# Last stage of a fused token mixer, retention and attention kernel: probabilities turned on VectorE in 32 by 32 blocks, value products in sixteen 32 by 32 tiles

## The reference

```python
x = layernorm(h)
gating = softmax(x @ W_gate.T)                       # 16 gates per token
idx, top1 = argmax(gating), max(gating)
q, k, v = split(x @ W_qkv.T, 3)
k_shared = k of head idx                             # (batch, 192, 32)
v_shared = top1 * (v of head idx)                    # (batch, 192, 32)
att = einsum('bhqd,bkd->bhqk', q, k_shared) / sqrt(32)
att = softmax(where(key <= query, att, -inf))
y = einsum('bhqk,bkd->bhqd', att, v_shared)
h = h + y.transpose(0, 2, 1, 3).reshape(batch, 192, 512)
```

## Time and profile before

| | |
|---|---|
| median of three runs | 1273.48 us |
| profiled execution, its own time | 1273.32 us |
| its span, first to last instruction | 1271.5 us |
| mean granted TensorE clock | 0.988 |
| busy share of the span: matmuls, weight loads, VectorE, ScalarE, GpSimd | 93, 77, 61, 44, 41% |
| one middle pair of the last stage, scores to scores | 52.3 us |

### The profile page before, as it was taken

One profiled execution on the slowest core, in us unless ns is written; L12 is line 12 of the kernel. 1 busy time (PEld: TensorE's weight loads), 2 busy tenths in 40 slices (PEclk: granted clock), 3 DMA queues, 4 the chain that ended last, 5 costly groups with the idle time before them and its releaser, 6 DMA issues. The chain is left out here.

```text
span 1271.5 us, 21324 instructions
## 1 busy us (share of the span) xinstructions
PE 1187.6 (93%) x7408; PEld 976.5 (77%) x7408; DVE 770.4 (61%) x1483; ACT 564.8 (44%) x1777; POOL 517.7 (41%) x714
## 2 busy tenths in 40 slices
PE   1689999999999999789999999998999999999997
PEld 1577788787887888678788887787887888888875
DVE  7897867678676742265555555634555655656544
ACT  6334333444424422253333333314556565565656
POOL 3576766747758651243233333302223212132131
PEclk9988999999999999989999999999999999999998
DMA  6022223222222222995667654133625527256061
GB/s 270 26 91 91 99 100 116 92 91 100 109 108 91 108 100 91 300 289 165 187 208 220 186 166 133 59 75 67 133 53 117 121 47 166 60 109 141 7 137 35
DMA packets 63354, 154.69 MB, mean 122 GB/s; under 512 B 9616, under 2 KB 26128, under 8 KB 61712
## 3 DMA queue, kind: packets, MB, share of 16 engines
q1 hardware_dynamic: 63248, 153.33, 41.3%
HBM read 67.19 MB, written 56.62 MB: 97 GB/s over the span
## 5 line engine op out<-in xcount | busy, mean ns | idle before, releaser
L1815 ACT ACTIVATE probs<-psum,row_max 128x128 f32<-128x128 f32 (+1 forms) x384 | 143.2, 389 | 41.5 <-DVE row_max L1984 29.2
L1119 ACT ACTIVATE square_scratch<-psum 128x128 f32<-128x128 f32 x192 | 51.0, 278 | 145.8 <-PE psum L1355 145.8
L1984 DVE TENSOR_REDUCE row_max<-psum 128x2 f32<-128x384 f32 (+1 forms) x128 | 79.1, 618 | 59.3 <-PE psum L2220 35.7
L2114 POOL TENSOR_TENSOR h_rows<-h_rows,y_normed 128x512 f32<-128x512 f32 x24 | 30.8, 1283 | 203.8 <-DVE y_normed L2000 203.8
L2091 POOL TENSOR_TENSOR picked_rows<-picked_rows 128x768 f32<-128x768 f32 (+1 forms) x64 | 61.4, 960 | 98.6 <-DVE picked_rows L1966 94.8
L753 POOL TENSOR_TENSOR stage<-stage 128x512 f32<-128x512 f32 x48 | 81.1, 1709 | 37.5 <-DVE stage L629 37.5
L1295 POOL TENSOR_TENSOR rr<-ss,consts_r 128x3 f32<-128x3 f32 x64 | 14.8, 231 | 188.6 <-ACT square_scratch L1119 184.0
L1991 DVE COPY raw_f<-psum 128x512 f32<-128x512 f32 x64 | 44.3, 692 | 70.2 <-PE psum L2233 70.2
L1815 ACT ACTIVATION_READ_ACCUMULATOR probs<-psum,row_max 128x1 f32 x384 | 80.9, 211 | 0.0
L798 PE MATMUL psum<-m,basis 128*128 128x64 f32 x384 | 49.1, 284 | 33.4 <-DVE basis L280 27.7
L1377 PE MATMUL psum<-wo_high,y_high 128*128 128x512 f32 x192 | 79.2, 412 | 1.0 <-issue 1.0
(11 more groups left out here) (281 smaller groups left out, 3584.8 us busy)
## 6 DMA issues: line engine op xcount, KB each, us to landing
qk<-stage SPq DMA_DIRECT2D x24, 512.0 KB, 2.6
v<-stage SPq DMA_DIRECT2D x24, 512.0 KB, 2.6
g<-gate_rows SPq DMA_DIRECT2D x24, 512.0 KB, 2.6
qk_rows<-qk SPq DMA_DIRECT2D x16, 512.0 KB, 6.5
q_stack_even<-q_t_high SPq DMA_DIRECT2D x32, 224.0 KB, 4.8
q_stack_even<-q_t_low SPq DMA_DIRECT2D x32, 224.0 KB, 6.9
q_stack_odd<-q_t_high SPq DMA_DIRECT2D x32, 224.0 KB, 5.5
q_stack_odd<-q_t_low SPq DMA_DIRECT2D x32, 224.0 KB, 7.0
```

Of the source, the lines that this page charges most:

```text
L1119: last = nc.scalar.activation(sqs[:, h % 2, t], psum[:, OB[h % 3], t * RV:(t + 1) * RV], ACT.Square, accum_out=ss[:, h % 2, t:t + 1])
L1815: last = nc.scalar.activation(pr[:, g % 2, c], psum[:, SB[g % 3], c], ACT.Exp, bias=mx[:, g % 3, x:x + 1], accum_out=dsum[:, t, h:h + 1])
L1984: V.reduce_max(mx[:, g % 3, 0:nh], psum[:, SB[g % 3], 0:nh * w].rearrange("p (h n) -> p h n", h=nh), AX, negate=True).then_inc(s_max.sem, 1)
L2114: G.tensor_tensor(h, h, yn[:, (NT * i + t) % 2].rearrange("p h f -> p (h f)"), ALU.add).then_inc(added.sem, 1)
```

## The change

The probabilities no longer go through TensorE and PSUM. VectorE turns them with one instruction per step, straight from `probs` to SBUF, each block of 32 x 32 in place: the partitions of block row a then hold 32 keys of key block b at the columns of the 32 queries of block a. `p_transposes` and both `pt_evac` are gone.

The products with the values follow that layout: for each block row a, each class c of four heads and each key block b that a query of a may see, a product of 32 keys, 32 value columns and 128 moving columns (32 queries of 4 heads), at rows 32 a and columns 32 c of the array, summed over b in PSUM bank `YB[a]`. Blocks over the diagonal are left out. For tile 0 or 1 these are 4 x (1 + 2 + 3 + 4) = 40 products in one block, in step 4 or 8; for tile 2 two blocks of 2 x (5 + 6 + 5 + 6) = 44 products, in step 12 and in step 0 of the next pair. Every partition group needs all values, so `v_shared` (one buffer now) is stored to DRAM and read back spread over the four groups by three DMAs, after a wait for the store.

Banks 2 to 5 now hold the products, so the scores have two banks instead of three: those of step g+2 wait for the exponentials of step g, at the start of step g. On VectorE the turn of step g comes first in step g, ahead of the row maximum of step g+2. The transposed logits move to another buffer.

```diff
-    SB = [0, 1, 2]
-    PTB = [3, 4]
-    YTB = 5
+    SB = [0, 1]
+    YB = [2, 3, 4, 5]
...
+    def place_of(n):
+        if n == FULL - 1:
+            return turned_even, 0
+        if n < FULL:
+            return (turned_even, 512 * n) if n < 4 else (turned_odd, 512 * (n - 4))
+        return (turned_even, 512 + T * 2 * (n - FULL)) if n < FULL + 4 else (turned_odd, T * 2 * (n - FULL - 4))
...
+    def four_heads(n, a, b):
+        m, at = place_of(n)
+        w = keys_of(n)
+        rows = slice(a * B, (a + 1) * B)
         if n < FULL:
+            return m[rows, at:at + HB * w].rearrange("p (h n) -> p h n", h=HB)[:, :, b * B:(b + 1) * B]
+        k = b * B
+        return m[rows, at:at + HB * w].rearrange("p (s k n) -> p s k n", s=2, n=R)[:, :, k // R:k // R + (5 if b < 4 else 2):4 if b < 4 else 1,
+                                                                                   k % R:k % R + B]
     def freed(g):
         i, n = divmod(g, NS_F)
...
+        return y_sum.at(i - 1, 3) if n < 4 else y_sum.at(i, (0, 1, 2)[(n >= 7) + (n >= 12)])
...
-        def v_swap(i):
+        def spread_v(i):
             sp.wait_ge(v_ready.sem, v_ready.at(i, 1))
+            sp.dma_start(d["v_f"].rearrange("k (t b) f -> b k t f", t=NT), vx[:, :, :]).then_inc(v_stored.sem, 16)
+            sp.wait_ge(v_stored.sem, v_stored.at(i, 1))
 
             sp.wait_ge(y_sum.sem, y_sum.at(i - 1, 0))
-            sp.dma_start(vs[0:R, i % 2], vx[R:P, i % 2, 2]).then_inc(v_swapped.sem, 16)
-            sp.dma_start(vs[R:P, i % 2], vx[0:R, i % 2, 2]).then_inc(v_swapped.sem, 16)
+            sp.dma_start(vr[i % 2][:, 0:8], d["v_f"][None, :, 0:8].to_broadcast((4, B, 8, FD))).then_inc(v_spread.sem, 16)
+            for s in range(2):
+                sp.dma_start(vr[i % 2][s * R:(s + 1) * R, 8:NB],
+                             d["v_f"][None, :, 8 + 2 * s:NB + 2 * s].to_broadcast((2, B, 2, FD))).then_inc(v_spread.sem, 16)
...
         def exps(g):
-            act.wait_ge(pt_sum.sem, pt_sum.at(0, g - 1))
+            act.wait_ge(p_turned.sem, p_turned.at(0, g - 1))
...
-        def pt_evac(g):
-            act.wait_ge(pt_sum.sem, pt_sum.at(0, g + 1))
-
-            act.wait_ge(y_sum.sem, freed(g))
-            nc.scalar.activation(slot_of(g % NS_F)[:, 0:3].rearrange("p h n -> p (h n)"), psum[:, PTB[g % 2], 0:3 * P], ACT.Copy
-                                 ).then_inc(pt_out_a.sem, 1)
...
         def y_evac(i, t):
-            act.wait_ge(y_sum.sem, y_sum.at(i, (t + 1) * NVT))
+            act.wait_ge(y_sum.sem, y_sum.at(i, t + 1 if t < 2 else NV))
             act.wait_ge(yr_sum.sem, yr_sum.at(i, t))
-            nc.scalar.activation(yT[:, :, :].rearrange("p c n -> p (c n)"), psum[:, YTB, :], ACT.Copy
+            nc.scalar.activation(yT[:, :, :].rearrange("p j (a n) -> p a j n", a=4),
+                                 psum[:, YB[0]:YB[3] + 1, 0:P].rearrange("p a (j n) -> p a j n", j=HB), ACT.Copy
...
-        def pt_evac(g):
-            dve.wait_ge(pt_sum.sem, pt_sum.at(0, g + 1))
+        def turn(g):
+            n = g % NS_F
+            dve.wait_ge(probs.sem, probs.at(0, g + 1))
 
             dve.wait_ge(y_sum.sem, freed(g))
-            V.tensor_copy(slot_of(g % NS_F).rearrange("p h n -> p (h n)"), psum[:, PTB[g % 2], :]).then_inc(pt_out_d.sem, 1)
+            V.transpose(slot_of(n), pr[:, g % 2, 0:len(heads_of(n)) * keys_of(n)]).then_inc(p_turned.sem, 1)
...
             g = NS_F * i + n
+            turn(g)
             if g + 2 < LAST:
                 row_max(g + 2)
-            if n < FULL:
-                pt_evac(g)
...
         def scores(g):
-            pe.wait_ge(probs.sem, probs.at(0, g - 2))
+            pe.wait_ge(probs.sem, probs.at(0, g - 1))
...
-        def p_transposes(g):
...
+        def products(i, t, v_block, classes, blocks):
+            for b in range(2 * NT):
+                for c in classes:
+                    for a in range(4):
+                        if b < blocks(a):
+                            n = FULL + 2 * c if t == 2 else 4 * t + c
+                            last = mm(psum[c * B:(c + 1) * B, YB[a], 0:P].rearrange("p (h n) -> p h n", h=HB),
+                                      vr[i % 2][a * B:(a + 1) * B, v_block(a, b)], four_heads(n, a, b),
+                                      start=b == 0, stop=b == blocks(a) - 1)
+            last.then_inc(y_sum.sem, 1)
...
         def values(i, j):
+            if j < NT:
+                pe.wait_ge(yt_out.sem, yt_out.at(i, j))
             if j == 0:
+                pe.wait_ge(v_spread.sem, v_spread.at(i, 1))
+            pe.wait_ge(p_turned.sem, p_turned.at(i, 4 * (j + 1)))
+            if j < 2:
+                products(i, j, lambda a, b: 4 * j + b, range(4), lambda a: a + 1)
             else:
+                products(i, 2, lambda a, b: 4 * (a // 2) + b if b < 4 else b + 4, range(2 * j - 4, 2 * j - 2),
+                         lambda a: 5 + a % 2)
...
             side(i, n, back, ahead, beyond)
-            p_transposes(g)
             if n == 0 and back:
                 values(i - 1, NV - 1)
-            if n in (3, 5, 7, 9):
-                values(i, n // 2 - 1)
-            if n == 12:
-                values(i, 2 * NVT)
+            if n in (4, 8, 12):
+                values(i, n // 4 - 1)
```

More of the change, by code:

```diff
@@ L1504, in stage_f @@
     NS_F = FULL + FH // 2
-    NVT = 2
-    NV = NT * NVT
+    NV = 4
+    B = 32
+    NB = 10
     qs_odd = sb("q_stack_odd", [P, FH, QW], F32R)
@@ L1515, in stage_f @@
     pr = sb("probs", [P, 2, 512])
-    lgT = sb("logits_t", [P, TP])
+    lg_first = sb("v_spread_odd", [P, TP])
+    vr_odd = lg_first[:, 0:NB * FD]
     qs_even = sb("q_stack_even", [P, FH, QW], F32R)
@@ L1528, in stage_f @@
     ksT = sb("k_stack_t", [P, 2, 2, T + P], F32R)
-    vx = sb("v_shared", [P, 2, NT, FD])
-    vs = sb("v_swapped", [P, 2, FD])
+    vr_even = sb("v_spread_even", [P, NB * FD])
+    vr = [m.rearrange("p (k f) -> p k f", k=NB) for m in (vr_even[:, :], vr_odd)]
     lg = sb("logits", [P, 5, NT, FH])
@@ L1639, in cols, with logits_t @@
         return slice((0, 2 * P, P)[t], (0, 2 * P, P)[t] + P)
+    def logits_t(i):
+        m = sel[:, 0, 0].rearrange("p h f -> p (h f)") if i else lg_first
+        return m[0:2 * FH, 0:TP]
     def tile_of(n):
@@ L1681, in sync @@
     def sync(sp):
-        for s in (*h_in, *stored, q_stacked, v_swapped):
+        for s in (*h_in, *stored, q_stacked, v_stored, v_spread):
             s.prime(sp)
@@ L1738, in run @@
             q_stack(0)
-            v_swap(0)
+            spread_v(0)
             rest()
@@ L1762, in scalar @@
     def scalar(act):
-        for s in (normed, x_high, lgt_out, lg_exp, q_high, kt_out, probs, pt_out_a, yt_out):
+        for s in (normed, x_high, lgt_out, lg_exp, q_high, kt_out, probs, yt_out):
             s.prime(act)
@@ L2140, in tensor @@
     def tensor(pe):
-        for s in (x_sum, lgt_sum, lg_sum, q_sum, k_sum, v_sum, kt_sum, s_sum, pt_sum, y_sum, yr_sum):
+        for s in (x_sum, lgt_sum, lg_sum, q_sum, k_sum, v_sum, kt_sum, s_sum, y_sum, yr_sum):
             s.prime(pe)
@@ L2165, in logit_rows @@
                 o = TP + t * 2 * FH
-                last = nc.tensor.transpose(psum[:, lg_bank(i), o:o + 2 * FH], lgT[0:2 * FH, cols(t)],
+                last = nc.tensor.transpose(psum[:, lg_bank(i), o:o + 2 * FH], logits_t(i)[:, cols(t)],
                                            ident[0:2 * FH, 0:2 * FH])
@@ L2219, in scores @@
                            start=(x, b) == (0, 0), stop=False, skip_group_check=True)
-                last = mm(psum[:, SB[g % 3], P:2 * P].rearrange("p (h n) -> p h n", h=2), identb[:, :],
+                last = mm(psum[:, SB[g % 2], P:2 * P].rearrange("p (h n) -> p h n", h=2), identb[:, :],
                           bcast(maskb[:, P:P + R], 1, 2), start=False, stop=True, skip_group_check=True)
             last.then_inc(s_sum.sem, 1)
-        def p_transposes(g):
-            n = g % NS_F
-            pe.wait_ge(probs.sem, probs.at(0, g + 1))
-            if g >= 2:
-                out, done = pt_signal(g - 2)
-                pe.wait_ge(out.sem, done)
-            bank = psum[:, PTB[g % 2], :].rearrange("p (h n) -> p h n", h=HB)
-            for x in range(HB if n < FULL else 3):
-                last = nc.tensor.transpose(bank[:, x], pr[:, g % 2, x * P:(x + 1) * P], ident[:, :])
-            last.then_inc(pt_sum.sem, 1)
+        def products(i, t, v_block, classes, blocks):
[8 more added lines that the diff above has]
+            last.then_inc(y_sum.sem, 1)
@@ L2236, in values @@
         def values(i, j):
-            t, half = divmod(j, NVT)
-            if half == 0:
-                pe.wait_ge(yt_out.sem, yt_out.at(i, t))
+            if j < NT:
+                pe.wait_ge(yt_out.sem, yt_out.at(i, j))
             if j == 0:
-                pe.wait_ge(v_ready.sem, v_ready.at(i, 1))
-            if j == 2 * NVT:
-                pe.wait_ge(v_swapped.sem, v_swapped.at(i, 1))
```

(20 more changed lines are left out.)

52 lines of the change are left out of this document (18 added, 34 removed).

## The result

The changed kernel takes **1251.02 us** (median of four runs, 1249.5 to 1255.25) against 1272.59 for the kernel before in the same session: ratio 0.9836, 95% interval 0.9809 to 0.9862. The forecast was 1240.5 in a range of 1230 to 1262: the sign and the main mechanism held, and 10.5 us of the expected gain are missing. The profiled execution took 1249.5 us with a span of 1247.7, 23.8 us less than the span before.

The account below looks back on a forecast made before the run. TensorE's issue was taken to bound pairs 0 to 6, the chain of scores, maximum and exponentials pair 7. Pairs 0 to 5 -27, pair 6 -4, pair 7 -2: -33 from 1273.3 gives 1240.5 us, range 1230 to 1262.

Parts of the forecast that it names:

- The transposes' removal: TensorE, each pair: 56 transposes go, 6.1 us, of which 5.45 is paid out; a middle pair at about 47.8 us.
- Pair 6: No logits chain, but it runs into ScalarE's pace at its end: -4 us.
- The value blocks: Products with the values on TensorE: 6.34 us a pair instead of 5.66, so +0.68; bounds 5.0 to 12.7.
- The longest sum sets a block: Value blocks: all array tiles run independently, so the most passes on one tile, 8 or 12, give 1.36 or 1.81 us.
- (a): Value blocks: four row groups on one column group halve each other's rate, 12.7 us a pair; 1287 us, chance 0.12.
- (b): Value blocks: issue at 50 ns a matmul sets the pace, 16.8 us a pair; 1313 us, chance 0.05.
- Rival (d): Scores' wait for exponentials in every step: a new stall eats the whole gain, 1273 us, chance 0.03.
- Rival (c): VectorE's turn is slow, 1.2 us, or held up by GpSimd; half the gain goes, 1257 us, chance 0.10.
- The idle time: TensorE idle about 1.0 us before the logits instead of 0.21, and 0.3 us before the first key projection.
- The spread values: Store and spread read-back by SP: ready about 1032.3, landed about 1040, needed in step 4 about 1044; cost nothing.
- Pair 7, "-2": Last pair, a chain of scores, maximum, exponentials: gains the transposes, loses in its longer last block; -2 us.
- The sum: Whole kernel: -4.5 us a pair, -27 for pairs 0 to 5, -33 in all.

Follow-up runs that it names:

- run 5: The kernel before with two score banks instead of three and nothing else of the change: 1275.42 us (ratio 1.0017).
- Run 7: The changed kernel with every VectorE turn made twice into the same place, a drain between: 1256.07 us (ratio 0.9871).
- Run 2: The changed kernel with the last value block of pairs 0 to 6 moved into their own step 15, its turn ahead of the last rows' split: 1248.87 us.
- run 10: The changed kernel with stacked queries first, last value block in step 15, its turn before the last pick, pair 7's first block in step 6, 48 idle products: 1235.34 us.
- run 3: The changed kernel with pair 7's first value block in step 6 instead of 4: 1245.39 us (ratio 0.979).
- run 4: The changed kernel with pair 7's first value block in step 6 and 48 products that feed nothing added in pair 7: 1246.44 us (ratio 0.9797).
- run 1: The changed kernel with SyncE issuing the stacked queries ahead of the three loads of rows: 1244.18 us (ratio 0.9778).
- run 6: The changed kernel with the value blocks above the diagonal multiplied too, 128 and 96 matmuls: 1255.59 us (ratio 0.9862).
- run 9: The changed kernel with blocks above the diagonal multiplied too, each product over 64 columns instead of 128: 1251.06 us.
- runs 8: The changed kernel with stacked queries ahead of the load of rows and the last value block in step 15: 1242.35 us (ratio 0.9762).

## Why the prediction was right, and where it was off

- **The transposes' removal** paid as worked out. Pair 5, without a gap, went from 52.3 to 47.4 us; the forecast was 47.8. With the blocks as measured below the working gives it: -5.45 + 0.25 + 0.3 = -4.9. Pair 6, forecast at -4 for a pace of ScalarE at its end, has only 0.24 us of such a wait: -6.1 + 0.25 + 0.3 + 0.24 = -5.3, as measured. The 0.7 us that pair 0 won beyond the working are not taken apart.
- **The value blocks.** Forecast 6.34 us a pair (two of 1.36, two of 1.81); measured from start to the next product 1.44 twice and 1.52 twice, 5.91. The total was near, the step behind it was half right: the blocks of sixteen tiles took more than forecast (1.36), those of eight less (1.81). "The longest sum sets a block" holds for tile 2, where eight tiles run and 88 and 96 matmuls take the same 1.322 us; the second pass starts 0.133 us after the first, as in the earlier trace rows, the later ones every 0.11 us. For sixteen tiles it fails: with the longest sum unchanged, 128 matmuls took 1.635 us where 80 took 1.236. Rounds of 32 at 13.5 ns a matmul give 4 x 0.433 - 0.11 = 1.62 for the 128. The same rule, each round the longer of two passes (0.22) and 13.5 ns a matmul, gives 0.43 + 0.32 + 0.22 + 0.22 - 0.11 = 1.08 for the 80, which is 0.15 short. So it describes full rounds and not the shrinking ones, and what sets the 13.5 ns is not settled by the runs.
- **Rivals (a) and (b)**, row groups that share and 50 ns a matmul, are dead: a block of 80 takes 1.44 us, not 2.7 or 4. The stretch of the earlier trace rows was no rate of issue. The Trainium skill ("TensorE: Matmul & The Clock Gate", section on 56 ns) gives about 62 ns of sequencer for each MATMUL with hardware decode off. That bound does not act on these blocks: 80 matmuls, with 80 weight loads, start within 1.236 us, 15.6 ns each. Whether hardware decode was on, no run shows. Of the chances, (a) and (b) add to 0.17 where "slower" has 0.15; the 0.02 that went to "faster" had no reason given.
- **Rival (d)**, a new stall in every step: the scores' wait on two banks cost nothing in pairs 0 to 5 (run 5).
- **Rival (c)**, the slow turn: dead. 0.70 and 0.57 us for forecasts of 0.65 and 0.50. Run 7 adds 9 us more of it at 0.5 us a pair. No lock with GpSimd shows in its times: in the changed kernel 47 of the 128 turns have a GpSimd instruction beside them for over half of their time, and they take 690 to 702 ns (512 columns) and 556 to 569 (384), where the others take 694 to 714 and 545 to 579.
- **The idle time** before the logits (0.9 for a forecast of 1.0) and before the first key projection (0.3 for 0.3) is where it was said to be. Run 2 wins half of the first back, run 10 nearly all (0.85 us a pair).
- **The spread values.** This step failed in pair 7. "SP has nothing else due: nothing" was argued for a middle pair alone, and the path was costed at 7.7 us (1032.3 to 1040), which is what it takes (7.9). Pair 7 has no side work, its steps are 1.4 to 2.5 us, and step 4 comes 7.8 us after its start (1211.88), not the 13.7 that the working allowed (1044 after 1030.3). The same sentence should have been asked of the pair without cover.
- **Pair 7, "-2"**, was the failed term: +8.5 us. Its parts, each from one execution and so rough: 5.1 for the late copy and the longer stay at the low clock (run 3; 3.1 of it is the idle time that the copy caused, the rest may hold up to 2.4 of chance), 0.8 net for the clock in what is left (run 4), 1.2 for two banks instead of three (run 5, in the kernel before; not isolated in the changed one), and the rest, 1.4, is not taken apart. The -2 also counted the removed transposes as a gain in a pair where TensorE waits for ScalarE; there they were not cost but work that kept the clock at 1.00 (48 products that feed nothing do the same in runs 4 and 10).
- **SyncE's queue** was not in the sum at all. "SP has nothing else due" was said of the time of the spread copy; the stacked queries, 14 us of issues and their landing, had some 2.5 us of slack when pairs took 52.3; the scores that want them came 4.8 us sooner, the issues only 1.3. 5.3 us in pairs 1 to 4; run 1 took them back by moving three issues.
- **The sum.** Without these gaps pairs 0 to 6 would have won 35 us, against a forecast of 31; the gaps took 5.3 of it, pair 7 turned -2 into +8.5, and 2.4 us of the profiled difference came before pair 0, where the clock differed at 104 us. -33 became -23.8 in the spans, and -21.6 in the medians.

## What to carry to other kernels

When a bound stage gets shorter, list every chain whose length does not shrink with it, DMA issues first, and compare its slack with the gain per iteration: here a queue with about 2.5 us to spare met a gain of 4.9. Cost each step a second time in the iteration that has no side work, since a copy that is hidden everywhere else stands bare there. Removed TensorE work in a stretch where the engine waits anyway is not a gain, and can lower its clock; check the granted clock of the last iteration before counting one.

## What was not expected of the hardware

- Sixteen 32 by 32 tiles run at once. In full rounds an fp32 matmul of 128 columns starts every 13.5 ns, weight load included (run 6), with 64 columns every 10 ns (run 9). With eight tiles a pass of 128 columns takes 0.11 us behind the first one, not the 0.134 of the earlier trace rows.
- TensorE's granted clock went from 1.00 to 0.50 in the changed kernel after gaps of 0.2, 1.1 and 0.6 us among products that fill some 3 of 4 us. With three more products in each step it stayed at 1.00 as long as TensorE had work (runs 4 and 10). It stayed at 0.50 from 1216 to 1232 us in the changed kernel, with TensorE busy for 3.6 to 4.0 of every 4 us.
- The time at the low clock varies between executions: pair 7 took 43.6 us in the changed kernel and 41.2 in run 1, whose code is the same there. It took 38.8 and 39.5 us in runs 8 and 2, which take one block out of its first step and leave the rest of it alone.
